# Layer norms of the batch after next taken in the fourth group, the next batch's q and k tiles a step sooner, and the openings' rows moved by ScalarE and SyncE side by side

## The chip, the cores and the metric

One NeuronCore of a Trainium2 chip runs the whole program. The metric is the device time of one execution in microseconds. The engines are TensorE (PE, with its weight loads PEld), VectorE (DVE), ScalarE (ACT), GpSimd (POOL) and SyncE (SP); SP, ACT and POOL also issue DMAs.

## The reference, cut to what matters

Input x is 4 batches of 512 tokens of 288 channels. Three transformer layers run one after the other, with a small rotation of the channels between the second and the third.

```python
mod = silu(c) @ w_adaln + b_adaln           # shift, scale, gate for attention and for the MLP
h   = (1 + sc_msa) * layernorm(x) + sh_msa
q, k, v = split_heads(h @ w_qkv + b_qkv)    # 16 heads of 18
o   = softmax(q @ k.T * 18 ** -0.5) @ v
x   = x + g_msa * (o @ w_proj + b_proj)
h   = (1 + sc_mlp) * layernorm(x) + sh_mlp
x   = x + g_mlp * mlp(h)                    # first layer: 4 experts, top 2; the others dense, 288 -> 1152 -> 288
```

## The kernel before

Everything is float32, with each large product made of high and low float32r parts. Attention is worked per layer, batch (0 to 3) and group of four heads (0 to 3). A group has four steps, one for each 128 keys. In each step `walk` calls on every engine the same sequence: two heads' tiles, place A, the other two heads' tiles, place B, the products of the step before with v, place C. The places hold everything that isn't a score tile, and `other_work` says what stands in which: "T1" turns the layer-normed rows `xn` of the next batch (PE L1065; ACT then makes `hTraw` and `hTh`, DVE `hTl`), "P" makes one of five tiles of the next batch's q and k rows (PE L1025, ACT L1513 the high part, DVE L1952 the low part), "V" makes v, "R" turns the maxima, "ot" turns the attention's output, "pj" is the projection, "LN1" and "LN2" are the layer norms (statistics on DVE, the rest on POOL, which writes the one buffer `xn`), "HH" is one Householder reflection of the rotation, which POOL works on beside the first two layers.

The softmax needs each row's maximum before the scores are exponentiated. So q k^T is made twice: the "max" tiles (PE L1123, reduced by DVE at L1970) run two groups ahead of the score tiles (PE L1136, exponentiated by ACT at L1560). While group 2 of a batch is scored, the maxima of group 0 of the next batch are found. Their q and k come through DRAM: SP stores the high and the low part of a tile in `qk_rows` (L494) and, when two tiles have landed, loads them stacked into `qs` and `ks` (L511, eight DMAs; "stack" g is for group g and needs tiles g and g + 1). SP works in the order of its code, and the negated maxima (`nmT` to `qs`, L518) go through the same queue.

Each layer opens without this overlap: T1, four P tiles, four V tiles, in the first and third layer also the rest of the modulation and its two gate rows (`gate_out`, ACT L1447, one row buffer `tmpx` in the third layer), and then the maxima of groups 0 and 1. In the opening the PSUM banks go round a ring of seven (`AROUND`). Where gate rows are made, the ring gives their two banks to the sixth and the seventh max tile, which therefore wait for ACT's copy of a gate row.

Of the kernel before, what the change touches and what calls it, by code (L numbers as in the profile page):

```python
# [78 lines left out]
def residuals_before(l):  # L79

    return TT * (0, 2, 2 + B)[l]
# [33 lines left out]
def other_work(g, kt, place, l, b):  # L115
    prev, nxt = b > 0, b + 1 < B
    work = {}
    for kt_, p, w in (
# [4 lines left out]
        0: [(0, "B", [("LN1a", 0)]), (0, "C", [("V", 0)]), (1, "A", [("LN1b", 0)]), (1, "B", [("V", 1)]), (1, "C", [("LN1c", 0)]),  # L123
            (2, "A", [("V", 2)]), (2, "C", [("V", 3)])] if b else
# [10 lines left out]
    for kind, arg in work.get((kt, place), []):  # L135
# [6 lines left out]
        if kind[:3] in ("T1", "LN1") and not nxt:  # L142
            continue
        if not b and g == 1 and (kind == "T1" or kind == "P"):
            continue
# [118 lines left out]
def bass_cond_seq_kernel(nc, a, out):  # L264
# [8 lines left out]
    with ExitStack() as ctx:  # L273
# [172 lines left out]

        @block.sync
        def _(sp):
# [19 lines left out]
            for l in range(NL):  # L468
# [17 lines left out]
                def store_tile(i, tile):  # L486
# [5 lines left out]
                    for part, done in enumerate(("hi_done", "lo_done")):  # L492
                        sp.wait_ge(S[done], i * QT + tile + 1)
                        sp.dma_start(qkd[o:o + QR[tile] // HD, part], qk[0:QR[tile], tile % 2, part, :].bitcast(F32)).then_inc(S[f"qk_st{tile % 2}"], 16)  # L494

                def stack(i, g):

                    if g == 0:
                        store_tile(i, 0)
                    store_tile(i, g + 1)  # L500
# [4 lines left out]
                    o = 2 * HG * g  # L505
                    for to, row, src in ((qs, 0, qkd[o:o + HG]), (qs, 2 * HD, qkd[o:o + HG, 0:1]), (ks, 0, qkd[o + HG:o + 2 * HG, 0:1]),
                                         (ks, HD, qkd[o + HG:o + 2 * HG])):
                        for e in range(2):
                            part = src.rearrange("(p e) a d n -> e (a d) p n", e=2)[e]
                            at = HALF * e + row  # L510
                            sp.dma_start(to[at:at + part.shape[0], i % 2, 2 * g:2 * g + 2, :].bitcast(F32), part).then_inc(S[f"stack_ld{g}"], 16)  # L511
# [15 lines left out]
                for b in range(B - 1):  # L527
                    for g in range(NG):
# [16 lines left out]
                        if g == 0 and b == 0:  # L545
                            stack(B * l, NG - 1)
# [1869 lines left out]
```

## Time and profile before

| what | value |
|---|---|
| median of 3 runs | 1769.82 us (1766.54 to 1772.14) |
| the profiled execution | 1758.09 us, of it 1756.3 us between first and last instruction |
| PE busy | 1604.5 us, 91% |
| DVE, ACT, POOL busy | 1100.8, 943.3 and 607.3 us |

The profiled execution is 11.7 us shorter than the median of the runs. A busy PE in such a page is not a PE at its peak, since pipelined matmuls are counted to their modelled ends; its idle time and the rows that say what ended it are read instead.

### The profile page before, as it was taken

What the parts mean: (1) busy time and instruction counts of PE and PEld (TensorE: products, weight loads), DVE (VectorE), ACT (ScalarE), POOL (GpSimd) and SP (SyncE); (2) the same over time, 40 slices, a digit from 0 to 9 for tenths busy, and PEclk for the clock granted to TensorE, in tenths of its full rate; (3) what the DMA queues carried; (4) which work ended last, traced back from release to release, by engine and by line L of the source; (5) the groups of instructions that cost most, each with busy time, mean ns of one, the idle gap of its engine ahead of it and who ended that gap; (6) DMA issues with size and microseconds to landing.
All of it is one profiled execution on the core that took longest, in us unless ns stands there. A gap on an engine that the chain in (4) does not pass through costs nothing.

```text
span 1756.3 us, 27872 instructions
## 1 busy us (share of the span) xinstructions
PE 1604.5 (91%) x9533; PEld 1050.5 (60%) x9533; DVE 1100.8 (63%) x2234; ACT 943.3 (54%) x1698; POOL 607.3 (35%) x1349
## 2 busy tenths in 40 slices
PE   6899989998989998998799899999987999998998
PEld 5334455446778887877335444479854454543897
DVE  4757667746545446473787777554457877784544
ACT  2466535565555455553366657744432766676442
POOL 1255665665255547572374552110001011201100
PEclk9799989999999999998699999999997999999999
DMA  6652423433373454441442212220204323222000
GB/s 196 194 138 89 155 101 123 163 110 120 120 246 130 142 184 144 156 143 41 143 127 81 93 58 90 72 59 1 46 4 131 99 81 93 67 91 72 18 28 28
DMA packets 100976, 183.44 MB, mean 104 GB/s; under 512 B 12078, under 2 KB 54457, under 8 KB 100723
## 3 DMA queue, kind: packets, MB, share of 16 engines
q1 hardware_dynamic: 90094, 145.97, 26.2%
q0 software_dynamic: 8352, 33.20, 6.1%
q10 hardware_dynamic: 2388, 2.48, 0.5%
q8 instruction: 77, 1.26, 0.3%
q14 instruction: 65, 0.52, 0.1%
HBM read 133.18 MB, written 60.05 MB: 110 GB/s over the span
## 4 chain that ended last, share of the span: by engine, by line
PE 63%; DMA 11%; DVE 9%; ACT 6%; issue 5%; SPq 3%; POOL 2%; ACTq 0%; DVEq 0%; POOLq 0%
PE ps L1284 13%; PE ps L1295 13%; PE ps L1147 7%; PE ps L1136 6%; PE ps L1025 5%; DMA qk_rows<-qk 4%; PE ps L1123 3%; DVE mx L1970 3%; PE ps L1076 3%; PE ps L1032 2%; DMA w2raw<-in_w 2%; ACT pT L1560 2%; SPq L511 2%; PE ps L1065 2%; DMA ks<-qk_rows 1%
## 5 line engine op out<-in xcount | busy, mean ns | idle before, releaser
L1970 DVE TENSOR_REDUCE mx<-ps 128x1 f32<-128x512 f32 x768 | 481.5, 681 | 70.9 <-PE ps L1123 68.7
L1560 ACT ACTIVATE pT<-ps 128x512 f32<-128x512 f32 x768 | 410.5, 601 | 190.5 <-PE ps L1136 189.8
L1123 PE MATMUL ps<-ks,qs 54*128 54x512 f32 x768 | 292.2, 489 | 39.4 <-DMA ks<-qk_rows 32.5
L1136 PE MATMUL ps<-qs,ks 56*128 56x512 f32 x768 | 274.4, 462 | 13.3 <-DMA qs<-nmT 4.7
L1904 DVE TENSOR_TENSOR gl<-gf,gh 128x512 fp32r<-128x512 f32 x171 | 118.8, 696 | 192.5 <-ACT gh L1474 191.4
L1136 PEld LDWEIGHTS ps<-qs,ks 56*128 56x128 f32 x768 | 119.0, 192 | 179.3 <-issue 98.4
L1147 PE MATMUL ps<-pT,vaug 128*32 128x512 f32 x1536 | 213.8, 625 | 5.9 <-ACT pT L1560 5.8
L1295 PE MATMUL ps<-w2h,gh 128*128 128x288 f32 x684 | 207.6, 304 | 2.8 <-DVE tmpx L2004 1.9
L1295 PE MATMUL ps<-w2l,gh 128*128 128x288 f32 x684 | 202.9, 297 | 0.0
L1295 PE MATMUL ps<-w2h,gl 128*128 128x288 f32 x684 | 202.2, 296 | 0.0
L753 POOL TENSOR_SCALAR nwp<-mvp 128x4 f32<-128x4 f32 x21 | 4.5, 212 | 543.8 <-DVE mvp L1791 543.6
L1123 PEld LDWEIGHTS ps<-ks,qs 54*128 54x128 f32 x768 | 124.3, 201 | 74.1 <-DMA ks<-qk_rows 37.3
L1295 PEld LDWEIGHTS ps<-w2h,gh 128*128 128x128 f32 x684 | 130.2, 190 | 10.6 <-issue 3.4
L1295 PEld LDWEIGHTS ps<-w2l,gh 128*128 128x128 f32 x684 | 130.5, 191 | 4.9
L1295 PEld LDWEIGHTS ps<-w2h,gl 128*128 128x128 f32 x684 | 130.2, 190 | 0.0
L1473 ACT ACTIVATE gf<-ps,b1t 128x512 f32<-128x512 f32 x99 | 67.7, 684 | 105.9 <-PE ps L1284 105.8
L1473 ACT ACTIVATE gf<-ps,cols 128x512 f32<-128x512 f32 x72 | 49.6, 689 | 126.4 <-PE ps L1284 126.1
L724 POOL TENSOR_TENSOR hs<-hR,hs 96x1 f32<-96x1 f32 x64 | 42.6, 666 | 208.7 <-ACT hR L1479 208.6
L1284 PE MATMUL ps<-hTh,w1h 128*128 128x512 f32 x252 | 105.0, 417 | 1.4 <-DVE hTl L1928 1.4
L1284 PE MATMUL ps<-hTl,w1h 128*128 128x512 f32 x252 | 100.9, 400 | 0.0
L1284 PE MATMUL ps<-hTh,w1l 128*128 128x512 f32 x252 | 100.7, 400 | 0.0
L1952 DVE SCALAR_TENSOR_TENSOR qk<-ps,cols,qk 126x512 fp32r<-126x512 f32 (+1 forms) x60 | 45.0, 750 | 87.8 <-ACT qk L1513 87.1
(292 smaller groups left out, 3076.5 us busy)
## 6 DMA issues: line engine op xcount, KB each, us to landing
qk_rows<-qk SPq DMA_DIRECT2D x96, 252.0 KB
w1raw<-in_w SPq DMA_DIRECT2D x39, 576.0 KB, 4.2
w2raw<-in_w SPq DMA_DIRECT2D x39, 432.0 KB, 4.9
qs<-qk_rows SPq DMA_DIRECT2D x96, 144.0 KB
ks<-qk_rows SPq DMA_DIRECT2D x96, 144.0 KB
expert_out<-expert_out POOLq DMA_DIRECT2D x8, 1152.0 KB, 6.2
htok<-expert_rows SPq DMA_DIRECT2D x11, 768.0 KB, 6.8
qs<-qk_rows SPq DMA_DIRECT2D x96, 72.0 KB
```

Source lines behind the costliest of these rows:

```text
L1025: ins = mm(ps[0:rows, n, :], w[:, c, o:o + rows], h[:, c, :], start=(c == 0 and k == 0), stop=(c == KC - 1))
L1076: ins = mm(ps[:, n, 0:C], oT[0:k, c, t * P:(t + 1) * P], wproj[0:k, c, :], start=(c == 0), stop=(c == KC - 1))
L1123: ins = mm(bank(n), qs[at:at + KMAX, buf, h // 2, qt * P:(qt + 1) * P], ks[at:at + KMAX, buf, h // 2, :], start=True, stop=True, tile_posi ...
L1136: ins = mm(bank(n), ks[at:at + KROW, b % 2, h // 2, kt * P:(kt + 1) * P], qs[at:at + KROW, b % 2, h // 2, :], start=True, stop=True, tile_ ...
L1147: ins = mm(ps[32 * i:32 * i + 32, 4, :], vaug[:, kt, g % NG * HG + i, :], pT[:, kt % 2 * HG + i, :], start=(kt == 0), stop=(kt == TT - 1), ...
L1284: ins = mm(bank(j % 3), w[:, c, o:o + P], h[:, c, :], start=(c == 0 and n == 0), stop=(c == KC - 1))
L1295: ins = mm(ps[:, 4 + t, 0:C], g[:, j % 3, t * P:(t + 1) * P], w[:, j, :], start=(j == 0 and n == 0), stop=(j == NJ - 1 and n == 2))
L1473: A(gf[:, j % 3, :], bank(j % 3), gelu, bias=bias)
L1560: A(pT[:, kt % 2 * HG + i, :], bank(BANK[when[0], "score", (g, kt, i)]), ACT.Exp, scale=SCALE).then_inc(S["exp_done"], 1)
L1904: V.tensor_tensor(gl[:, j % 3, :], gf[:, j % 3, :], gh[:, j % 3, :].bitcast(F32), ALU.subtract).then_inc(S["gl_done"], 1)
L1952: V.scalar_tensor_tensor(out=qk[0:rows, slot, 1, :], in0=ps[0:rows, BANK[when[0], "P", tile], :], scalar=cols[0:rows, l, tile:tile + 1], i ...
L1970: V.tensor_reduce(mx[:, g % NG, qt, column(i):column(i) + 1], bank(BANK[when[0], "max", (g, qt, i)]), AX.X, ALU.max).then_inc(S["mx_done"], 1)
```

## The change

Three things change. First, in batches 1 and 2 the T1 turns for the next batch leave group 1 and stand in group 0 (steps 2 and 3), the V tiles of group 0 move up a little, and P 0 and P 1 stand in step 0 of group 1 instead of step 1. For this the layer norm must be ready earlier: it is taken in group 3 for the batch after next (batches 0 and 1 do it) instead of in group 0 for the next one (batches 1 and 2). Second, SP stores tiles 0 and 1 ahead of the maxima of group 2. Third, in the openings ACT stores the high parts of tiles 0 to 3 and loads the q half of stacks 0 and 1, while SP stores the low parts and loads the k half; the ones rows (`put_ones`) go to the queue later.

```diff
     own = {
-        0: [(0, "B", [("LN1a", 0)]), (0, "C", [("V", 0)]), (1, "A", [("LN1b", 0)]), (1, "B", [("V", 1)]), (1, "C", [("LN1c", 0)]),
-            (2, "A", [("V", 2)]), (2, "C", [("V", 3)])] if b else
+        0: [(0, "C", [("V", 0)]), (1, "A", [("V", 1)]), (1, "C", [("V", 2)]), (2, "A", [("V", 3)]), (2, "B", [("T1", 0)]), (2, "C", [("T1", 1)]),
+            (3, "B", [("T1", 2)])] if b else
            [(0, "B", [("T1", 0)]), (0, "C", [("T1", 1)]), (1, "A", [("T1", 2)]), (1, "C", [("P", 0)]), (2, "C", [("P", 1)])],
-        1: [(0, "A", [("T1", 0)]), (0, "B", [("T1", 1)]), (0, "C", [("T1", 2)]), (1, "A", [("P", 0)]), (1, "B", [("P", 1), ("pj", 0)]),
+        1: [(0, "A", [("P", 0)]), (0, "C", [("P", 1)]), (1, "B", [("pj", 0)]),
...
-            (2, "C", [("T0", 1)]), (3, "A", [("T0", 2)]), (3, "B", [("pos", 0)])],
+            (2, "C", [("T0", 1)]), (3, "A", [("T0", 2)]), (3, "B", [("pos", 0)]), (0, "B", [("LN1a", 0)]), (1, "A", [("LN1b", 0)]), (1, "C", [("LN1c", 0)])],
...
-        if kind[:3] in ("T1", "LN1") and not nxt:
+        if kind == "T1" and not nxt or kind[:3] == "LN1" and b + 2 >= B:
...
                 G0 = NG * B * l
                 sp.wait_ge(S["oT_ones"], l + 1)
+                store_tile(B * l, 0, (1,))
+                store_tile(B * l, 1, (1,))
+                stack(B * l, 0, (1,))
+                store_tile(B * l, 2, (1,))
+                stack(B * l, 1, (1,))
                 put_ones(0)
+                store_tile(B * l, 3, (1,))
+                stack(B * l, 2)
                 put_ones(1)
-                stack(B * l, 0)
-                stack(B * l, 1)
-                stack(B * l, 2)
...
+                        if g == 1 and b:
+                            store_tile(i, 0)
+                            store_tile(i, 1)
...
                     for tile in range(QT - 1):
                         high_part(it, tile)
+                        act.wait_ge(S["hi_done"], it * QT + tile + 1)
+                        act.dma_start(*rows_of(tile, 0)).then_inc(S[f"qk_st{tile % 2}"], 16)
+                        if tile % 2:
+                            g = tile // 2
+                            for n in (g, g + 1):
+                                act.wait_ge(S[f"qk_st{n % 2}"], stored(it, n))
+                            load_rows(act, it, g, 0)
                     if l != 1:
                         for u in range(2):
                             gate_out(l, u, BANK[when[0], "G", (l, u)])
```

The first place is ACT's queue in the opening of the third layer, from the third high part on. Before, these rows stand there:

```order
L1513 ACTIVATE qk<-ps,cols 126x512 [waits qk_st0,qk_mm]
L1513 ACTIVATE qk<-ps,cols 126x512 [waits qk_st1,qk_mm]
L1447 ACTIVATE tmpx<-ps 4x288 [waits mod_stored1,gate_mm]
L1449 DMA mod_rows<-tmpx 4x288 [waits gate_cp]
L1447 ACTIVATE tmpx<-ps 4x288 [waits mod_stored2,gate_mm]
L1449 DMA mod_rows<-tmpx 4x288 [waits gate_cp]
```

After, with the loads of `qs` for stack 0 (second half of them) ahead of the third high part and those for stack 1 ahead of the gate rows:

```order
L459 DMA qs<-qk_rows 36x2x512
L459 DMA qs<-qk_rows 18x2x512 x2
L1534 ACTIVATE qk<-ps,cols 126x512 [waits qk_st0,qk_mm]
L1647 DMA qk_rows<-qk 7x18x512 [waits hi_done]
L1534 ACTIVATE qk<-ps,cols 126x512 [waits qk_st1,qk_mm]
L1647 DMA qk_rows<-qk 7x18x512 [waits hi_done]
L459 DMA qs<-qk_rows 36x2x512 [waits qk_st0,qk_st1]
L459 DMA qs<-qk_rows 36x2x512
L459 DMA qs<-qk_rows 18x2x512 x2
L1468 ACTIVATE tmpx<-ps 4x288 [waits mod_stored1,gate_mm]
L1470 DMA mod_rows<-tmpx 4x288 [waits gate_cp]
L1468 ACTIVATE tmpx<-ps 4x288 [waits mod_stored2,gate_mm]
```

Both gate rows now stand behind a wait for rows stored in DRAM (`qk_st0`, `qk_st1`), and so does the third high part.

The second place is ACT's queue in the third layer, batch 1, where group 0 ends and group 1 begins (`hTraw` and `hTh` are T1's, `oT` is "ot", `oc` closes the group before, `qk` is a P tile). Before:

```order
L1535 ACTIVATE hTraw<-ps,modcol 128x512
L1540 ACTIVATE hTh<-hTraw 128x512
L1552 ACTIVATE oc<-ps 128x512
L1535 ACTIVATE hTraw<-ps,modcol 128x512
L1540 ACTIVATE hTh<-hTraw 128x512
L1560 ACTIVATE pT<-ps 128x512 x2
L1520 ACTIVATE nmT<-ps 8x512
L1513 ACTIVATE qk<-ps,cols 126x512
L1560 ACTIVATE pT<-ps 128x512 x2
L1513 ACTIVATE qk<-ps,cols 126x512
```

After:

```order
L1556 ACTIVATE hTraw<-ps,modcol 128x512
L1561 ACTIVATE hTh<-hTraw 128x512
L1567 ACTIVATE oT<-ps 96x512
L1581 ACTIVATE pT<-ps 128x512 x2
L1534 ACTIVATE qk<-ps,cols 126x512
L1581 ACTIVATE pT<-ps 128x512 x2
L1573 ACTIVATE oc<-ps 128x512
L1534 ACTIVATE qk<-ps,cols 126x512
L1581 ACTIVATE pT<-ps 128x512 x2
L1541 ACTIVATE nmT<-ps 8x512
```

The T1 pairs now stand ahead of `oc`, in group 0 and among its `oT` copies, and the two P rows follow within the first step of group 1.

The third place is SP's queue in group 1 of the third layer, batch 1. Before:

```order
L518 DMA qs<-nmT 2x2x512 [waits nmT_ready]
L518 DMA qs<-nmT 2x2x512
L494 DMA qk_rows<-qk 7x18x512 [waits hi_done,stack_ld0]
L494 DMA qk_rows<-qk 7x18x512 [waits lo_done]
L494 DMA qk_rows<-qk 7x18x512 [waits hi_done,stack_ld1,stack_ld0]
L494 DMA qk_rows<-qk 7x18x512 [waits lo_done]
L511 DMA qs<-qk_rows 36x2x512 [waits st_mm,qk_st1,qk_st0]
L511 DMA qs<-qk_rows 36x2x512
```

After:

```order
L508 DMA qk_rows<-qk 7x18x512 [waits hi_done,stack_ld0]
L508 DMA qk_rows<-qk 7x18x512 [waits lo_done]
L508 DMA qk_rows<-qk 7x18x512 [waits hi_done,stack_ld1,stack_ld0]
L508 DMA qk_rows<-qk 7x18x512 [waits lo_done]
L524 DMA qs<-nmT 2x2x512 [waits nmT_ready]
L524 DMA qs<-nmT 2x2x512
L459 DMA qs<-qk_rows 36x2x512 [waits st_mm,qk_st1,qk_st0]
L459 DMA qs<-qk_rows 36x2x512
```

The four stores moved ahead of the two DMAs of maxima; the loads stayed behind both.

## Rows read from the trace of the kernel before

**Rows 1.** Waits of PE: engine and line, waited for: total us, times, longest us.

```profile
PE ps L1123 <- DMA ks<-qk_rows: 32.5, 12, 9.3
...
PE ps L1025 <- DVE hTl L1961: 4.1, 5, 0.9
```

**Rows 2.** Busy time by stretch: groups 1 and 2 together (four times), group 0, group 3.

```profile
core 0: us, PE busy (x) PEld busy (x) DVE busy (x) ACT busy (x) POOL busy (x), PEclk, DMA share, GB/s
944.10:988.40 44.30, 40.28 (x231) 20.91 (x230) 30.69 (x61) 28.19 (x54) 25.37 (x80) 1.00 0.24 77
1020.10:1067.00 46.90, 44.72 (x231) 22.76 (x230) 31.02 (x61) 28.55 (x54) 24.00 (x77) 0.89 0.23 72
1429.80:1475.10 45.30, 41.10 (x223) 21.25 (x222) 30.85 (x61) 27.56 (x50) 4.40 (x9) 0.92 0.25 75
1505.40:1547.30 41.90, 39.17 (x221) 19.91 (x221) 30.73 (x61) 27.42 (x50) 4.41 (x9) 1.00 0.25 81
1488.30:1505.40 17.10, 17.00 (x118) 9.10 (x114) 15.50 (x36) 10.60 (x21) 4.40 (x9) 1.00 0.24 71
1547.30:1560.60 13.30, 13.16 (x85) 5.30 (x81) 11.50 (x22) 9.88 (x20) 0.00 (x0) 1.00 0.35 108
```

**Rows 3.** Busy time by stretch, ten us around a stack wait in layer 2.

```profile
1044.00:1054.00 10.00, 8.80 (x30) 3.94 (x27) 5.72 (x15) 3.42 (x7) 7.92 (x23) 0.59 0.13 38
```

**Rows 4.** Chain that ended last, third layer, batch 2, groups 1 and 2: start, us.

```profile
1515.20 1.65 PE ps L1025 x7
...
1518.44 6.13 DMA qk_rows<-qk
...
1527.21 3.85 DMA ks<-qk_rows
...
1531.11 0.51 PE ps L1123 x2
...
1539.14 0.59 PE ps L1065 x4
```

**Rows 5.** Timeline of ACT, third layer, batch 2, start of group 1.

```profile
1507.75 0.63 ACT L1540 ACTIVATE hTh<-hTraw 128x512 fp32r<-128x512 f32 x1
1508.29 1.07 ACT L1560 ACTIVATE pT<-ps 128x512 f32<-128x512 f32 x2
1509.24 0.78 ACT L1535 ACTIVATE hTraw<-ps,modcol 128x512 f32<-128x512 f32 x1
```

**Rows 6.** Timeline of SP's queue, opening of the third layer.

```profile
1325.13 1.47 SPq L511 DMA_DIRECT2D qs<-qk_rows  x4
...
1334.83 1.45 SPq L511 DMA_DIRECT2D qs<-qk_rows  x4
```

**Rows 7.** Timeline of ACT, the same opening.

```profile
1325.16 0.69 ACT L1513 ACTIVATE qk<-ps,cols 126x512 fp32r<-126x512 f32 x1 [2.18 <-DMA qk_rows<-qk]
1328.62 0.40 ACT L1447 ACTIVATE tmpx<-ps 4x288 f32<-4x288 f32 x1 [2.78 <-PE ps L939]
...
1333.22 0.40 ACT L1447 ACTIVATE tmpx<-ps 4x288 f32<-4x288 f32 x1 [4.19 <-DMA mod_rows<-tmpx]
```

**Rows 8.** Timeline of DVE, the same opening.

```profile
1325.88 0.75 DVE L1952 SCALAR_TENSOR_TENSOR qk<-ps,cols,qk 126x512 fp32r<-126x512 f32 x1 [2.12 <-ACT qk L1513]
1326.54 1.54 DVE L1983 TENSOR_TENSOR vaug<-ps,vbias 128x288 f32<-128x288 f32 x4
...
1328.36 1.53 DVE L1786 BATCH_NORM_STATS2 stats<-xres 128x6 f32<-128x288 f32 x4
...
1332.09 9.65 DVE L1970 TENSOR_REDUCE mx<-ps 128x1 f32<-128x512 f32 x16 [1.68 <-PE ps L1123]
```

**Rows 9.** Timeline of PE, the same opening.

```profile
1333.67 4.74 PE L1123 MATMUL ps<-ks,qs 54*128 54x512 f32 x10 [1.15 <-ACT tmpx L1447]
```

**Rows 10.** Timeline of DVE, opening of the second layer.

```profile
841.25 9.65 DVE L1970 TENSOR_REDUCE mx<-ps 128x1 f32<-128x512 f32 x16 [2.51 <-PE ps L1123]
...
852.51 0.69 DVE L1970 TENSOR_REDUCE mx<-ps 128x1 f32<-128x512 f32 x1 [1.19 <-PE ps L1123]
```

More of the change, by code:

```diff
@@ L141, in other_work @@
             continue
-        if kind[:3] in ("T1", "LN1") and not nxt:
+        if kind == "T1" and not nxt or kind[:3] == "LN1" and b + 2 >= B:
             continue
-        if not b and g == 1 and (kind == "T1" or kind == "P"):
+        if not b and g == 1 and kind == "P":
             continue
@@ L445, in load_ada, with rows_of, load_rows @@
             eng.dma_start(to[CW:CW + 1, KC - 1, at:at + n * C], a["w_ada"][l][C:C + 1, src]).then_inc(S[sem], 16)
+        def rows_of(tile, part):
+            return qkd[HT * tile:HT * tile + QR[tile] // HD, part], qk[0:QR[tile], tile % 2, part, :].bitcast(F32)
+        def load_rows(eng, i, g, which):
+            o = 2 * HG * g
+            for to, row, src in (((qs, 0, qkd[o:o + HG]), (qs, 2 * HD, qkd[o:o + HG, 0:1])),
+                                 ((ks, 0, qkd[o + HG:o + 2 * HG, 0:1]), (ks, HD, qkd[o + HG:o + 2 * HG])))[which]:
+                for e in range(2):
+                    part = src.rearrange("(p e) a d n -> e (a d) p n", e=2)[e]
+                    at = HALF * e + row
+                    eng.dma_start(to[at:at + part.shape[0], i % 2, 2 * g:2 * g + 2, :].bitcast(F32), part).then_inc(S[f"stack_ld{g}"], 16)
         @block.sync
@@ L484, in _, with store_tile @@
                     sp.wait_ge(S["ys_done"], 16 * TILES)
-                def store_tile(i, tile):
+                def store_tile(i, tile, parts=(0, 1)):
                     o = HT * tile
@@ L491, in store_tile, with stack @@
                             sp.wait_ge(S[f"stack_ld{g}"], i * 128)
[L492 to L500, printed above, removed]
+                    for part in parts:
+                        sp.wait_ge(S[("hi_done", "lo_done")[part]], i * QT + tile + 1)
+                        sp.dma_start(*rows_of(tile, part)).then_inc(S[f"qk_st{tile % 2}"], 16)
+                def stack(i, g, which=(0, 1)):
                     for tile in (g, g + 1):
@@ L504, in stack @@
                         sp.wait_ge(S["st_mm"], NU * (NG * (i - 2) + g + 1))
[L505 to L511, printed above, removed]
+                    for part in which:
+                        load_rows(sp, i, g, part)
                 def maxima(G, g):
@@ L521, in _ @@
                 sp.wait_ge(S["oT_ones"], l + 1)
+                store_tile(B * l, 0, (1,))
[3 more added lines that the diff above has]
+                stack(B * l, 1, (1,))
                 put_ones(0)
+                store_tile(B * l, 3, (1,))
+                stack(B * l, 2)
                 put_ones(1)
[L524 to L526 removed]
                 for b in range(B - 1):
+                    i = b + (B * l + 1)
                     for g in range(NG):
@@ L774, in others @@
                         if kind == "LN1c":
-                            normalise(1, it + 1, b + 1, EPS[l], (("tr1_done", it * KC + KC), ("tr2_done", it * KC + KC)))
+                            normalise(1, it + 2, b + 2, EPS[l], (("tr1_done", it * KC + 2 * KC), ("tr2_done", it * KC + 2 * KC)) + ((("lg_tr", it),) if l == 0 and b else ()))
                         elif kind == "LN2c":
@@ L1615, in start @@
                         split_high(c, it)
+                    if l:
+                        act.wait_ge(S["fc2_mm"], NJ * units_before(l) + 3)
+                        act.wait_ge(S["xm_done"], residuals_before(l))
+                        for g in range(NG):
+                            act.wait_ge(S[f"stack_ld{g}"], it * 128)
+                    if l == 2:
+                        act.wait_ge(S["xr_done"], TT * B)
                     for tile in range(QT - 1):
                         high_part(it, tile)
+                        act.wait_ge(S["hi_done"], it * QT + tile + 1)
[5 more added lines that the diff above has]
+                            load_rows(act, it, g, 0)
                     if l != 1:
@@ L2030, in others @@
                         elif kind[:3] == "LN1":
-                            statistics(1, it + 1, b + 1, kind[3])
+                            statistics(1, it + 2, b + 2, kind[3])
                         elif kind == "pj":
```

15 lines of the change are left out of this document (11 added, 4 removed).

## The prediction

> **What bounds the kernel now.** I read the waits of TensorE first, then the busy time by stretch, then the chain that ended last, then the timelines of the openings. Among the waits one is far ahead: TensorE's max tiles wait 32.5 us in 12 places for rows of q and k that come back from DRAM [rows 1]. They fall in two kinds of places. In the three openings nothing hides the way through DRAM, and in batches 1 and 2 of the second and third layer the maxima of the next batch's group 0 start group 2, and its rows have just been asked for. The chain shows why: P 1 ends 1.65 us after 1515.20, then come high part, low part and SP's store, 6.13 us until the store has landed, eight loads, 3.85 us until the last one has landed, and the max tile at 1531.11 [rows 4]. From P 1's end to that tile are 14.3 us, whatever TensorE does meanwhile. Groups 1 and 2 together take 44.3, 46.9, 45.3 and 41.9 us in these four batches, with the same instructions on TensorE but for the reflections of the second layer [rows 2]. Part of the spread is the clock: around one of the waits the granted clock was 0.59, so for much of these ten us TensorE stood at 1.2 GHz, after it had idled [rows 3].
>
> **The change part by part, groups 1 and 2.** P 1 moves from the second step of group 1 to its first. Before it stand now two pairs of tiles, P 0, v's products and P 1 itself, an estimated 6.2 us from the group's start; with the 14.3 us of the chain the stack is there at 20.5 us. Without T1 the group's own work is about 20.7 us, so at most some tenths of a wait remain. To price it I start at the calmest batch, 41.9 us at full clock [rows 2]. The gap between the last load's issue, its 3.85 us, and the tile [rows 4] left TensorE idle for 1.7 us; that goes. T1 is three turns of 0.59 us, read at a turn of the same shape [rows 4], 1.8 us. P 0 no longer waits for `hTl`, five such waits of 0.8 us on the average, and its surroundings [rows 1], 1.0 us. So 41.9 - 1.7 - 1.8 - 1.0 = 37.4 us, and the same for the third layer's batch 1, since it has the same work. In the second layer I add 1.5 us, as POOL's reflections there hold TensorE in group 2 whatever the rows do: 38.9 us. Gains: 44.3 - 38.9, 46.9 - 38.9, 45.3 - 37.4, 41.9 - 37.4, together 25.8 us. The first layer had no such wait, and I set its groups 1 against its groups 0 and 3 at nothing (bounds -4 and +4): its batches are slowed by other work.
>
> **Group 0.** It gets T1: 1.8 us on TensorE, which was already busy for 17.00 of 17.10 us [rows 2]. On ScalarE each turn costs 0.78 + 0.63 us [rows 5], three of them 4.2 us, and all three stand in the second half of the group beside eight exponentials of 0.54 us (4.3 us) and the `oT` copies. That is more than the 8.5 us of half a group, so exponentials and with them v's products come late. I take 2.4 us for each of four batches, 9.6 us. Lower bound 1.0 (TensorE's gap at the start of the group swallows part), upper bound 4.2 (ScalarE's work in full).
>
> **Group 3.** The statistics, 1.53 us for four [rows 8] and 0.4 us for their aggregation, move to group 3 in batches 0 and 1. DVE was busy for 11.50 of 13.30 us there [rows 2] and each max tile needs it; it was busy for 15.50 of 17.10 us in group 0 too, but there `hTl` takes the place of the statistics. I take 1.0 us for each of four groups, 4.0 us, between 0 and 2. POOL's part is hidden by two or three steps in which nobody asks for `xn`.
>
> **The openings.** The low part of tile 1 sets the landing, and it is made no sooner, so the stores gain nothing (in the second layer the four DMAs of ones no longer stand ahead of them, about 1 us). The loads do: q's four cost 1.47 us of issuing ahead of k's four [rows 6], and now both go side by side. But ScalarE now stands in this queue. From the landing, 1325.13 in the third layer, it issues loads for 1.5 us, then makes the third high part, stores it, makes the fourth, 3.8 us in all. DVE follows with the low part (0.75), v (1.54), the modulation (0.5) and the statistics (1.9) [rows 8] and reaches the first maximum 8.6 us after the landing, at 1333.7 instead of 1332.09. These 1.6 us I take for the first layer too.
>
> The third layer loses more. The sixth and seventh max tile need the banks of the gate rows. The seventh already waited 1.15 us for the second copy [rows 9], because both copies share one row buffer and 4.19 us pass until the first has landed [rows 7]. Now both stand behind the second wait for stored rows. Low part 2 is made at 1328.1, the store lands some 6.4 us later, 1334.5; loads to 1336.0, first gate 1336.4, its row landed 1340.7, second gate 1341.1, seventh max tile and DVE from 1341.5. Ten more reductions of 0.6 us end at 1347.6 instead of 1341.75: 5.9 us later, and DVE is what the steps behind wait for. In the second layer there are no gates: DVE starts about 0.9 us sooner, and the 1.19 us for stack 1 [rows 10] vanish, 2.0 us gained. Openings: 1.6 - 2.0 + 5.9 = +5.5 us, between 0 (if the second landing is quick) and +9.
>
> The Trainium skill (Trainium Kernel Development and Optimization, Key Constraints) says that DMAs of all issuing engines run on the same 16 DMA engines and that several issuers only save "the sequencer's issue time". By that rule the gain of an opening is one times 1.47 us as above, and the sum stays; were the landings halved as well, each opening would be some 3 us better. No row here shows two queues at once on these rows.
>
> **Sum.** -25.8 + 9.6 + 4.0 + 5.5 = -6.7 us. On the profiled execution that is 1758.1 - 6.7 = 1751.4 us. The median of the runs shown lies 11.7 us above that execution; with the same difference taken off, 1769.8 - 6.7 = 1763.1 us.
>
> **The rivals.**
> *The openings don't lose.* If the second landing takes 4 us instead of 6.4 and the gate row's 2 instead of 4.2, the third opening costs 1.3 us and the first nothing: 5 to 6 us less, 1757 us. For it: those landings were timed with other rows in flight. Against: they still are. Chance 0.17.
> *Nothing is left.* Work moves between groups, and where DVE and TensorE were both nearly full it comes back in full: groups 0 at 4 us, groups 3 at 1.2 make +20.8 instead of +13.6, sum 0, 1770 us. For it: TensorE busy for 17.00 of 17.10 us. Against: groups 1 were full as well and lose the same work. Chance 0.16.
> *Slower, by ScalarE in group 0.* T1's copies stand among exponentials that feed v's products, DVE waits for `hTh` ahead of the maxima, and the ring of banks fills. It happens in batches 1 and 2 of all three layers, so six times. Beyond my 2.4 us each further us costs 6 us; from 4.4 us a group on the whole is slower by over 0.3%, at 5 us it gives 1769.8 - 6.7 + 6 x 2.6 = 1779 us. For it: 8.5 us of ScalarE and more in 8.5 us. Against: the same copies stood in one step and a half of group 1 before. Chance 0.17.
> *The forecast*, between -13 and -1 us: 0.50.
>
> **How the numbers follow.** A measurement of this kernel tells about 0.3%, 5.3 us, from no change. The forecast lies just beyond it: of its 0.50 some 0.32 is faster and 0.17 within. The first rival is faster. "Nothing is left" gives 0.03 faster, 0.10 within, 0.03 slower; the slower rival 0.13 slower, 0.04 within. Together faster 0.53, within 0.30, slower 0.17. The range takes the first rival's end and half of the slower one: 1751 to 1776 us.
>
> **What would show it.** Right: the stack waits at the start of group 2 gone and the granted clock there near 1.00; groups 1 and 2 at 37 to 39 us; groups 0 at 19 to 20 us; in the third opening DVE idle for about 3.5 us after its sixth reduction, with the second `tmpx` copy near 16 us after the first landing. Wrong: a wait for `ks` still standing in group 2 (P 1 came not soon enough, or the store took longer), idle time of TensorE at v's products in group 0, or waits for `nmT` at the start of group 3, since group 2 is now short and SP brings the maxima behind stack 1's loads.

## The result, and the profile after

The changed kernel takes 1786.56 us (median of 4 runs, 1784.34 to 1789.86) where the kernel before took 1770.43 us beside it: ratio 1.0096, 95% interval 1.0073 to 1.0119. That is 17 us slower, outside the range on record (1751 to 1776 us), and the other way than forecast. A second set of runs, on another chip, gave 1.0097 (1.0056 to 1.0138).

The two profiled executions lie 31.8 us apart (spans 1756.3 and 1788.1 us), because the one of before was the fastest seen by then and the one of the change the slowest of its four. So the rows say where time is spent, the ratios how much counts. A second profile of before, below, helps to tell a draw from an effect.

Engine totals on the page after the change: TensorE is busy for 25 us more with the same 9533 matmuls, the first sign of a lower clock.

```profile
PE 1629.5 (91%) x9533; PEld 1057.9 (59%) x9533; DVE 1103.6 (62%) x2234; ACT 945.0 (53%) x1698; POOL 610.0 (34%) x1349
```

The waits of TensorE, changed kernel (engine and line, waited for: total us, times, longest us):

```profile
PE ps L1144 <- DMA qs<-qk_rows: 12.4, 3, 8.6
PE ps L999 <- POOL hr L731: 9.9, 3, 3.9
...
PE ps L1144 <- ACT tmpx L1468: 9.1, 2, 6.1
```

The max tiles' 32.5 us in 12 places [rows 1] have become 12.4 us in 3, all in openings: the stack waits at the start of group 2 are gone, as forecast. But these four waits were only 6.9 of the 32.5 us; the rest belonged to the openings. Here they are on TensorE's timeline of the kernel before, the second layer's two and the third layer's two:

```profile
969.61 0.50 PE L1123 MATMUL ps<-ks,qs 54*128 54x512 f32 x2 [0.94 <-DMA ks<-qk_rows]
1045.88 0.80 PE L1123 MATMUL ps<-ks,qs 54*128 54x512 f32 x2 [1.20 <-DMA ks<-qk_rows]
1456.96 0.80 PE L1123 MATMUL ps<-ks,qs 54*128 54x512 f32 x2 [3.13 <-DMA ks<-qk_rows]
1531.11 0.51 PE L1123 MATMUL ps<-ks,qs 54*128 54x512 f32 x2 [1.67 <-DMA ks<-qk_rows]
```

Two other waits stand out in the changed kernel: 9.9 us for `hr`, which is POOL's part of a reflection, and 9.1 us for `tmpx`, the gate rows. In the kernel before they were:

```profile
PE ps L978 <- POOL hr L710: 2.1, 1, 2.1
...
PE ps L1123 <- ACT tmpx L1447: 1.1, 1, 1.1
```

Busy time by stretch, changed kernel: groups 1 and 2 together of the same four batches as [rows 2], then group 0 and group 3 of the third layer, and group 0 of the first layer's batch 1.

```profile
core 0: us, PE busy (x) PEld busy (x) DVE busy (x) ACT busy (x) POOL busy (x), PEclk, DMA share, GB/s
965.70:1012.00 46.30, 42.81 (x219) 21.55 (x218) 29.50 (x58) 24.59 (x49) 24.20 (x77) 0.89 0.24 73
1048.30:1091.90 43.60, 40.43 (x217) 20.64 (x216) 28.49 (x57) 24.32 (x48) 22.24 (x73) 0.96 0.24 78
1467.90:1506.70 38.80, 37.67 (x209) 18.76 (x208) 29.62 (x59) 23.66 (x44) 4.41 (x9) 1.00 0.28 87
1540.10:1578.40 38.30, 37.58 (x209) 18.73 (x208) 29.15 (x58) 23.54 (x44) 4.41 (x9) 1.00 0.28 88
1520.20:1540.10 19.90, 19.07 (x130) 10.38 (x126) 15.58 (x30) 14.60 (x27) 0.00 (x0) 1.00 0.20 61
142.30:170.80 28.50, 23.75 (x132) 12.33 (x128) 17.24 (x40) 15.12 (x29) 17.27 (x43) 0.82 0.34 106
1506.70:1520.20 13.50, 13.02 (x79) 5.42 (x79) 12.51 (x30) 9.69 (x19) 4.42 (x9) 1.00 0.36 106
```

The third layer came to 38.8 and 38.3 us at a full clock (forecast 37.4). The second layer came to 46.3 and 43.6 us, at a clock of 0.89 and 0.96 (forecast 38.9). POOL is busy for over 22 us there (24 and 25 us before [rows 2]), for 4.4 us in the third layer: what it does more in the second layer are the reflections.

**Where POOL holds TensorE.** POOL's timeline of the changed kernel, at the turn from batch 0 to batch 1 in the first layer: the end of one reflection, the layer norm "LN1c", the next reflection's first and last step.

```profile
133.62 0.31 POOL L731 TENSOR_TENSOR hr<-hp 96x59 f32<-96x59 f32 x1
135.81 0.20 POOL L774 TENSOR_SCALAR nwp<-mvp 128x4 f32<-128x4 f32 x1 [1.88 <-DVE mvp L1826]
...
137.81 2.28 POOL L781 TENSOR_SCALAR xn<-xres,nwp 128x288 f32<-128x288 f32 x4
140.16 0.51 POOL L784 COPY xn<-xn 128x384 f32<-128x384 f32 x1
140.64 0.56 POOL L745 TENSOR_TENSOR hs<-hR,hs 96x1 f32<-96x1 f32 x1
...
147.47 0.30 POOL L731 TENSOR_TENSOR hr<-hp 96x58 f32<-96x58 f32 x1
```

The product that hands this reflection over on TensorE, ScalarE's copy of it for POOL, and TensorE's next product of a reflection:

```profile
136.78 0.46 PE L999 MATMUL ps<-hr,ones 96*96 96x128 f32 x2
...
137.63 0.29 ACT L1500 ACTIVATE hR<-ps 96x128 f32<-96x128 f32 x1
...
147.88 0.71 PE L999 MATMUL ps<-hr,ones 96*96 96x128 f32 x2 [3.92 <-POOL hr L731]
```

The copy was there at 137.92. POOL was free at 133.93, waited 1.88 us for the statistics of the layer norm, which stands ahead of the reflection in its code, and took up the reflection at 140.64, 2.7 us late. The layer norm takes 4.8 us, a reflection 7.1 us, and two steps of group 3 about 7 us: TensorE stands still for 3.92 us, and the stretch behind runs at a mean clock of 0.82. In the kernel before the same product waited 1.5 us, for DVE.

In group 2 of the second layer's batch 1 the pattern is the same, but the layer norm in it is LN2c, which the change did not move. POOL's row 991.14 is its start, 995.99 and 1001.74 are the next reflection's first and last step:

```profile
991.14 0.20 POOL L774 TENSOR_SCALAR nwp<-mvp 128x4 f32<-128x4 f32 x1
...
995.99 0.56 POOL L745 TENSOR_TENSOR hs<-hR,hs 96x1 f32<-96x1 f32 x1
...
1001.74 0.20 POOL L731 TENSOR_TENSOR hr<-hp 96x9 f32<-96x9 f32 x1
```

```profile
1002.04 0.71 PE L999 MATMUL ps<-hr,ones 96*96 96x128 f32 x2 [3.15 <-POOL hr L731]
```

This product is the one that waited 2.1 us before (at 982.3 us in that trace). The third wait for `hr`, 2.8 us, is its counterpart in batch 2.

**Where the gate rows hold DVE.** The third opening on ScalarE, to set beside [rows 7]:

```profile
1350.30 1.57 ACTq L459 DMA_DIRECT2D qs<-qk_rows  x4
1351.97 0.69 ACT L1534 ACTIVATE qk<-ps,cols 126x512 fp32r<-126x512 f32 x1 [8.72 <-issue]
...
1361.01 1.54 ACTq L459 DMA_DIRECT2D qs<-qk_rows  x4
1362.65 0.40 ACT L1468 ACTIVATE tmpx<-ps 4x288 f32<-4x288 f32 x1 [8.43 <-issue]
...
1369.53 0.40 ACT L1468 ACTIVATE tmpx<-ps 4x288 f32<-4x288 f32 x1 [6.48 <-DMA mod_rows<-tmpx]
```

The same stretch on DVE, to set beside [rows 8]:

```profile
1359.65 3.08 DVE L2005 TENSOR_REDUCE mx<-ps 128x1 f32<-128x512 f32 x5 [0.86 <-PE ps L1144]
1363.93 0.69 DVE L2005 TENSOR_REDUCE mx<-ps 128x1 f32<-128x512 f32 x1 [1.19 <-PE ps L1144]
1370.81 4.28 DVE L2005 TENSOR_REDUCE mx<-ps 128x1 f32<-128x512 f32 x7 [6.18 <-PE ps L1144]
```

DVE idles where it was forecast to, after its sixth maximum, but for 6.18 us instead of 3.5. The second copy stands 19.2 us behind the first loads (1369.53 against 1350.30); 16 us was forecast. A second profile of the changed kernel (after_2 below) has 18.2 us there, with 5.72 us in place of the 6.48.

### The profile page after: what moved, and what is told of

It reads as the page before. It is cut to its first block, busy times and chain, and to the rows that moved or that the text cites. A ratio compares the mean times of both kernels' runs of the same rounds, so it can differ in the third digit from the quotient of the medians.

```text
span 1788.1 us, 27886 instructions
## 1 busy us (share of the span) xinstructions
PE 1629.5 (91%) x9533; PEld 1057.9 (59%) x9533; DVE 1103.6 (62%) x2234; ACT 945.0 (53%) x1698; POOL 610.0 (34%) x1349
## 4 chain that ended last, share of the span: by engine, by line
PE 63%; DVE 11%; DMA 9%; ACT 6%; issue 4%; POOL 4%; SPq 2%; ACTq 1%; another core or an unknown queue 0%; DVEq 0%; POOLq 0%
PE ps L1305 12%; PE ps L1316 12%; PE ps L1168 7%; PE ps L1157 6%; PE ps L1046 5%; DVE mx L2005 5%; PE ps L1097 4%; DMA qk_rows<-qk 4%; PE ps L1144 3%; DMA w2raw<-in_w 2%; PE ps L1053 2%; PE ps L1086 2%; ACT qk L1534 1%; PE ps L1067 1%; PE ps L1060 1%
## 5 line engine op out<-in xcount | busy, mean ns | idle before, releaser
L1144 PE MATMUL ps<-ks,qs 54*128 54x512 f32 x768 | 300.6, 492 | 33.2 <-DMA qs<-qk_rows 12.4
L1157 PE MATMUL ps<-qs,ks 56*128 56x512 f32 x768 | 278.3, 463 | 16.0 <-DMA qs<-nmT 4.4
L1168 PE MATMUL ps<-pT,vaug 128*32 128x512 f32 x1536 | 218.1, 633 | 6.6 <-ACT pT L1581 6.6
L1144 PEld LDWEIGHTS ps<-ks,qs 54*128 54x128 f32 x768 | 126.1, 202 | 73.5 <-DVE mx L2005 23.5
```

What stands on the lines that cost most here:

```text
L1144: ins = mm(bank(n), qs[at:at + KMAX, buf, h // 2, qt * P:(qt + 1) * P], ks[at:at + KMAX, buf, h // 2, :], start=True, stop=True, tile_posi ...
L1157: ins = mm(bank(n), ks[at:at + KROW, b % 2, h // 2, kt * P:(kt + 1) * P], qs[at:at + KROW, b % 2, h // 2, :], start=True, stop=True, tile_ ...
L1168: ins = mm(ps[32 * i:32 * i + 32, 4, :], vaug[:, kt, g % NG * HG + i, :], pT[:, kt % 2 * HG + i, :], start=(kt == 0), stop=(kt == TT - 1), ...
```

## The experiments

The tables below give the time from the first score tile of a group to that of the next, read in each kernel's timeline. Ratios are to the kernel before on the same chip. The median of the kernel before moved between 1762 and 1774 us from chip to chip, so only ratios are compared. Each interval reaches 0.2 to 0.4% to either side, and a difference of two ratios is uncertain by an estimated 0.3 to 0.5%: many of the conclusions rest on the traces, and the ratios say whether they add up.

**The kernel before again.**

> The kernel before, unchanged, for a second profile of it and for the spread: ratio 1.000 within 0.003. If the profiled execution shown in front (11.7 us below the median of the runs) was a lucky one, this profile has its stack waits in the same 12 places but a span near 1768 us.

Ratio 0.9990 (0.9958 to 1.0022), the profiled span 1760.9 us, again at the low end of its runs: the page's execution was no great exception. It waits 23.6 us in 10 places for stacks, where the same 12 places had been expected. The group times of the two profiles show what is fixed and what is a draw. In the second layer group 1 of batch 2 took 24.1 us in both; group 2 took 20.2 and 23.2 us in batch 1, 22.8 and 19.9 us in batch 2; group 0 of the first layer's batch 3 took 17.6 and 21.1 us. So [rows 2] had bad draws, and the first layer's 17.6 us was a good one.

**The openings alone.** The order of work of before, with the third part of the diff only:

```diff
+                store_tile(B * l, 0, (1,))
+                store_tile(B * l, 1, (1,))
+                stack(B * l, 0, (1,))
...
-                put_ones(1)
-                stack(B * l, 0)
-                stack(B * l, 1)
...
```

> The kernel before with only the third change: in the openings ScalarE stores the high parts and loads the q half of stacks 0 and 1, SyncE the rest, ones rows later. Order of work in the groups and of stores there as before. Theory one (the openings cost what the two traces show between T1 and the first score tile: +2.9, -1.3 and +10.6 us): about 12 us slower than before, 9 to 15; in the third layer the second gate row is copied some 19 us after the first loads are issued, and DVE is idle for over 5 us among the maxima of group 0. Rival (most of the loss comes from the moved work, and what an opening loses comes back behind it): at most 5 us slower.

Ratio 1.0042 (1.0019 to 1.0065), 7.5 us, which lies between both theories, and 1.0063 (1.0027 to 1.0098), 11 us, on another chip, which lies within the first. From the first maximum to the first score tile the third opening took 25.4 and 26.1 us, against 17.9 and 18.4 in the two profiles of before. The second opening got no slower.

**The moved work alone.** The table of places and the order of stores as in the change, the opening as before:

```diff
-                        act.dma_start(*rows_of(tile, 0)).then_inc(S[f"qk_st{tile % 2}"], 16)
-                        if tile % 2:
...
-                            load_rows(act, it, g, 0)
```

> The changed kernel with the opening of the kernel before: SyncE alone stores and loads, ones rows first. Theory one (openings cost 12 of the 16 us): 2 to 6 us slower than before, since what groups 1 and 2 gain (11 us by the traces) is lost again in groups 0 and 3 and by reflections that wait for GpSimd. Rival one (the forecast's own terms without the openings): 12 us faster. Rival two (the moved work is the cause): over 9 us slower.

Ratio 1.0048 (1.0029 to 1.0067), 8.5 us, more than theory one's 2 to 6 us and just under rival two. 0.42% and 0.48% add up to nearly all of the 0.96%: two faults, about equal as far as the intervals tell, that hardly meet. Here the waits for `hr` are 9.9 us, as in the changed kernel.

**Gate rows freed.** ScalarE no longer waits for stack 1's rows:

```diff
-                stack(B * l, 1, (1,))
+                stack(B * l, 1)
...
-                        if tile % 2:
-                            g = tile // 2
+                        if tile == 1:
+                            g = 0
```

> The changed kernel, but ScalarE loads only the q half of stack 0; SyncE loads stack 1 in full, so that in the first and third layer the gate rows no longer stand behind a wait for stack 1's stored rows. Theory one (that wait holds the gate rows, and these the sixth and seventh max tile): the first gate row is copied as soon as TensorE has made it, the third opening is 5 to 9 us shorter, and the kernel 5 to 9 us faster than the changed one, 7 to 11 us slower than before. Rival (the landing of the first gate row, 6.5 us, is what counts, wherever it starts): 0 to 3 us faster than the changed one.

Ratio 1.0053 (1.0027 to 1.0080), 0.43% or 7.6 us under the changed kernel, as theory one has it. ScalarE and DVE in the third opening:

```profile
1345.08 1.57 ACTq L459 DMA_DIRECT2D qs<-qk_rows  x4
...
1351.36 0.40 ACT L1468 ACTIVATE tmpx<-ps 4x288 f32<-4x288 f32 x1 [2.35 <-PE ps L960]
...
1356.31 0.40 ACT L1468 ACTIVATE tmpx<-ps 4x288 f32<-4x288 f32 x1 [4.54 <-DMA mod_rows<-tmpx]
```

```profile
1354.49 9.65 DVE L2005 TENSOR_REDUCE mx<-ps 128x1 f32<-128x512 f32 x16 [0.92 <-PE ps L1144]
```

The second copy is made 11.2 us behind the first loads instead of 19.2, and DVE reduces all sixteen tiles in one go. First maximum to first score tile: 18.4 us, as before, against 26.0 us in the changed kernel.

**Do the 7 us count?** The same cure on the openings alone:

> The kernel before with the new openings, but ScalarE loads only the q half of stack 0. Order of work and reflections as before. Theory (two queues at once save an opening nothing that counts; the gate rows were all of the openings' loss in the third layer): maximum to first score tile in the third opening 18.4 us again (25.4 with the fault), time within 4 us of before. Rival (sharing the queues gains 1.5 us an opening once the gate rows are free): 3 to 5 us faster than before.

Ratio 1.0037 (1.0012 to 1.0062), only 0.05% under the openings alone on the other chip, though its third opening took 18.4 us. At 6.5 us over before it was a miss, so four kernels were run side by side on one chip.

> The changed kernel again, on one chip with the next three, to settle what the openings cost. Ratio to before 1.008 to 1.011 in either theory; its maximum to first score tile in the third opening takes 25 to 26 us.

> The changed kernel with the gate rows free of the wait for stack 1, again. Theory (the 7 us which the trace shows in the third opening are in the time in full): 0.3 to 0.5% under the changed kernel of the same call. Rival (part of them is given back by shorter groups behind the opening): under 0.2%.

> Only the new openings, again. Theory (openings cost the gate rows' 7 us and a little): 0.4 to 0.6% over before. Its partner is the next kernel, which had 1.0037 on another chip where this one had 1.0042; if the 7 us count in full they must lie 0.3 to 0.5% apart here.

> Only the new openings, with the gate rows free, again. Theory (the 1.0037 was a draw at the edge of its interval): 1.000 to 1.002. Rival (beside the gate rows the new openings cost something else, some 5 us, that no row has shown yet): 1.003 or more again.

Measured: 1.0097, 1.0044 (1.0013 to 1.0075), 1.0063, 1.0027 (0.9996 to 1.0057). The two differences are 0.53% and 0.36%, 9 and 6 us. With the 0.43% and the 0.05% of the earlier pairs the mean is 0.34%, 6 us: the gate rows' 7 us of the trace count, most of them at least; whether in full the intervals don't tell. Open_free's second ratio lies between its theory (up to 1.002) and its rival (1.003). Whether the new openings cost a little beside the gate rows (0.27% and 0.37% in these two, 0.05% where the moved work stands beside them) stays open; no gain of theirs shows in any ratio.

**Reflections made cheap.** In both kernels eight steps of POOL's reflection are left out or replaced, so that the rotation becomes the identity and the kernels compute without it:

```diff
-                step(g.tensor_tensor(nrm, sig, half, ALU.pow))
-                step(g.tensor_scalar(sg, al, 0.0, 2.0, ALU.is_ge, ALU.mult))
-                step(g.tensor_scalar(sn, sg, nrm, nrm, ALU.mult, ALU.subtract))
+                step(g.tensor_scalar(sn, al, 0.0, 1.0, ALU.mult, ALU.mult))
...
-                    step(g.tensor_tensor(rest, rest, outer(row, RD - 1 - j), ALU.subtract))
```

> The kernel before with a shorter reflection on GpSimd: eight of its steps are left out or replaced by a multiplication by zero, so the rotation becomes the identity; everything else stands. A control for the next kernel. GpSimd's part of a reflection falls from about 6.5 to 4 us. Theory (reflections bind a few places before too, such as the 2.1 us at 982.3): 3 to 10 us faster than before. Rival: nothing waits for them: within 3 us.

> The changed order of work with the opening of before and the same shorter reflection. Theory one (the layer norm moved into group 3 stands on GpSimd between two reflections, and group 2, now free of its wait for the stack, waits for GpSimd instead): against the kernel before with the same shorter reflection it is no slower, -4 to +2 us, where with full reflections it was 8.5 us slower; TensorE's waits for GpSimd (3 to 4 us each) are gone. Rival (the loss is ScalarE's and TensorE's, by the layer-norm turns in group 0): still 6 to 10 us slower than that control.

Ratios 0.9907 (0.9873 to 0.9941) and 0.9899 (0.9865 to 0.9933). The control's 16 us were far more than the 3 to 10 expected: reflections cost the kernel before more than its one wait of 2.1 us for `hr` shows. With full reflections the moved work was 0.48% slower than its control, with short ones it is 0.08% faster. Its waits for `hr` are gone. The second layer, groups 1 and 2 of batch 1 and group 2 of batch 2, first of the control and then with the moved work:

```profile
943.20:967.30 24.10, 23.33 (x128) 12.88 (x126) 17.63 (x33) 15.20 (x29) 4.91 (x18) 1.00 0.24 76
967.30:985.50 18.20, 17.20 (x106) 8.28 (x102) 13.12 (x29) 12.85 (x26) 8.39 (x27) 1.00 0.28 85
...
1041.30:1059.60 18.30, 17.25 (x108) 8.32 (x104) 13.14 (x29) 12.88 (x26) 8.25 (x27) 1.00 0.28 88
```

```profile
948.50:970.70 22.20, 22.20 (x118) 11.61 (x116) 16.10 (x31) 11.48 (x24) 4.12 (x18) 1.00 0.28 88
970.70:987.80 17.10, 16.75 (x108) 8.09 (x104) 13.07 (x29) 12.73 (x25) 8.39 (x27) 1.00 0.29 84
...
1045.10:1062.20 17.10, 16.74 (x108) 8.07 (x104) 13.07 (x29) 12.72 (x25) 8.25 (x27) 1.00 0.29 85
```

Group 2 falls to the 17.1 us of the third layer, and groups 1 and 2 to 39.3 us, the forecast's 38.9 almost. But the control, with its stack wait in place, needs only 42.3 us. Its group 2 takes 18.2 us against 17.1, both at a clock of 1.00: there the wait was worth 1.1 us, not 5 to 8. In the third layer, without any reflection, group 2 took 17.8 to 21.8 us in 14 instances of the old order and 16.9 to 17.7 us in 22 with the early P tiles: there it was worth 3 us on the mean, the fall of the clock included (0.84 in the 21.7 us of the kernel before).

**Reflections moved.** The moved work with full reflections at other steps:

```diff
-FWD_STEP = {(0, 0): (2, 5, 7, 9, 11, 14), (0, 1): (0, 2, 5, 7, 10, 12, 14), (0, 2): (0, 2, 5, 7, 10, 12, 14), ...
-            (1, 1): (0, 2, 4, 6, 8, 10, 12), (1, 2): (0, 2, 4, 6, 8, 10, 12)}
+FWD_STEP = {(0, 0): (2, 5, 7, 9, 11, 14), (0, 1): (1, 3, 5, 7, 10, 12, 14), (0, 2): (1, 3, 5, 7, 10, 12, 14), ...
+            (1, 1): (0, 2, 4, 7, 10, 12, 14), (1, 2): (1, 3, 5, 7, 10, 12, 14)}
```

> The changed order with the opening of before and full reflections, but where batches take a layer norm in group 3 the reflections stand at other steps (in the first layer's batches 1 and 2 and the second layer's batch 2 at 1, 3, 5, 7, 10, 12, 14, in its batch 1 at 0, 2, 4, 7, 10, 12, 14). Theory one (GpSimd's chain of reflection, layer norm, reflection is what group 2 and the start of the next batch wait for): 5 to 9 us faster than with the old steps, so 0 to 4 us slower than before. Rival (GpSimd only shares the blame with the turns in group 0): 0 to 3 us faster than with the old steps.

Ratio 0.9993 (0.9963 to 1.0023), 0.55% or 9.7 us under the same kernel with the old steps, which ran on another chip; theory one had 5 to 9 us. The wait that is left, in the list of waits:

```profile
PE ps L999 <- POOL hr L731: 3.7, 2, 2.0
```

The kept traces say the same of the second layer without any ratio. From the first score tile of batch 1 to that of batch 3 it takes 151.6 to 154.7 us in the eight profiles with the old order and full reflections at the old steps, 157.3 to 161.3 us in the five with the moved order, 154.9 and 155.1 us where the reflections are shifted too (moves_shift and repaired), and 148.1 and 148.6 us in the two short kernels. Shifted steps with the old order were run for the second layer alone (third_shift below, 151.8 and 151.6 us); what they would give the old order in the first layer was not run.

**Both repairs.** Gate rows freed and reflections moved, the rest as in the change.

> The whole change with both repairs: ScalarE loads only the q half of stack 0 (so that the gate rows are free), and the reflections stand at the shifted steps. Theory (the two faults add up, 0.43% for the gate rows and 0.55% for the reflections, and are all of the change's 0.96%): 1.000 of before, 0.996 to 1.003. Rival (they overlap, since each also lowers the granted clock where the other waits): 1.004 or more.

Ratio 0.9998 (0.9974 to 1.0022): within 0.24% the two faults are the whole of the 0.96%, and what is left of the change neither gains nor loses.

**The third layer alone.** The order of work chosen per layer:

```diff
+    early = l == 2
...
-        1: [(0, "A", [("P", 0)]), (0, "C", [("P", 1)]), (1, "B", [("pj", 0)]),
+        1: ([(0, "A", [("P", 0)]), (0, "C", [("P", 1)]), (1, "B", [("pj", 0)])] if early else
+            [(0, "A", [("T1", 0)]), (0, "B", [("T1", 1)]), (0, "C", [("T1", 2)]), (1, "A", [("P", 0)]), (1, "B", [("P", 1), ("pj", 0)])]) + [
```

> The changed order of work in the third layer alone; first and second layer and all openings as before. No reflections run in the third layer. Theory one (the moved work gains where no reflection stands beside it: layer 3 took 266.8 us before and 262.5 us with the moves): 3 to 6 us faster than before. Rival (group 0's loss cancels the gain there too): within 2 us of before.

Ratio 0.9997 (0.9968 to 1.0026), so not told from no change, nor from the low end of the 3 to 6 us expected. Its third layer took 262.3 us, against 266.9 and 266.6 in the profiles of before. The same without the earlier P tiles:

```diff
-        1: ([(0, "A", [("P", 0)]), (0, "C", [("P", 1)]), (1, "B", [("pj", 0)])] if early else
+        1: ([(1, "A", [("P", 0)]), (1, "B", [("P", 1), ("pj", 0)])] if early else
```

> In the third layer alone the layer norms and the T1 turns are moved as in the change, but P 0 and P 1 stay in the second step of group 1. Theory (only the earlier P tiles shorten group 2; the turns cost group 0 a little more than they give back in group 1): batches 1 and 2 of the third layer have groups 0 of 19.8 us, groups 1 of 21 to 22, and groups 2 still wait for the stack and take 18 to 21 us, so the layer takes 267 to 270 us. Rival (a shorter group 1 without T1 is what counts): groups 2 at 17 us without any earlier P.

Ratio 0.9997 (0.9970 to 1.0024), third layer 262.8 us. The layer's expected 267 to 270 us was a miss. Batch 1, groups 0, 1 and 2:

```profile
1418.60:1438.40 19.80, 18.97 (x128) 10.36 (x124) 15.53 (x30) 14.53 (x27) 0.00 (x0) 1.00 0.30 91
1438.40:1459.00 20.60, 20.60 (x113) 11.06 (x111) 15.82 (x30) 11.17 (x22) 0.00 (x0) 1.00 0.28 88
1459.00:1478.20 19.20, 17.80 (x104) 8.19 (x100) 13.57 (x30) 12.68 (x23) 4.41 (x9) 0.91 0.27 82
```

Group 2 still idles for 1.4 us and its clock falls to 0.91, yet the three groups take 59.6 us, against 60.0 us with the early P tiles, whose group 0 was one at a clock of 0.94. Groups 1 and 2 alone take 39.7 us against 39.0 in batch 1 and 38.3 us in either kernel in batch 2. With the turns gone from group 1, P comes early enough by itself for most of the effect; putting it a step sooner is worth under 1 us a batch here.

**A better version?** The third layer's moved work, and the second layer as before but with its reflections at 0, 2, 4, 7, 10, 12, 14.

> The candidate for a better version: the moved work in the third layer alone, and in the second layer, whose work stands as before, the reflections of batches 1 and 2 at steps 0, 2, 4, 7, 10, 12, 14 in place of 0, 2, 4, 6, 8, 10, 12. Theory (third layer 4 us shorter, groups 2 of the second layer 1 to 3 us shorter since TensorE waited for GpSimd there): 5 to 9 us faster than before. Rival (what a group saves there is within the spread of the second layer's batches): 0 to 4 us faster.

> The candidate (moved work in the third layer alone, shifted reflections in the second) once more, since its first interval, 0.9961 to 1.0014, holds both no change and the 5 us expected. Theory: 0.996 to 0.999. Rival: 0.999 or more, and no better version is shown.

Ratios 0.9987 (0.9961 to 1.0014) and 0.9980 (0.9954 to 1.0005), medians of 1757.54 and 1758.18 us beside 1763.25 and 1762.09 us for before. The mean is 0.9983, about 3 us; each interval holds 1, so it is the best candidate and not shown to be faster; the 5 to 9 us expected of it are missed. Its second layer's groups 2 took 18.9 and 18.6 us (before: 20.2 and 23.2, 22.8 and 19.9), but its groups 1 rose from 24.1 to 24.7 us and its groups 3 from 13.8 to 14.6 and 14.4.

| us, group 0 / 1 / 2 | before | before again | changed | moves, short | moves, shifted | third alone |
|---|---|---|---|---|---|---|
| 2nd layer, batch 1 | 17.9 / 24.1 / 20.2 | 18.0 / 24.1 / 23.2 | 21.1 / 22.1 / 24.1 | 21.1 / 22.1 / 17.1 | 21.1 / 22.8 / 20.3 | 18.0 / 24.1 / 20.2 |
| 2nd layer, batch 2 | 17.9 / 24.1 / 22.8 | 17.9 / 24.1 / 19.9 | 22.7 / 22.2 / 21.4 | 21.1 / 22.1 / 17.1 | 20.3 / 22.6 / 18.6 | 18.0 / 24.1 / 19.9 |
| 3rd layer, batch 1 | 17.0 / 23.5 / 21.7 | 17.0 / 23.5 / 21.5 | 19.8 / 21.4 / 17.4 | 19.9 / 21.4 / 17.0 | 21.4 / 21.4 / 17.0 | 21.1 / 21.6 / 17.3 |
| 3rd layer, batch 2 | 17.0 / 23.6 / 18.4 | 17.0 / 23.5 / 20.7 | 19.8 / 21.4 / 17.0 | 19.8 / 21.4 / 17.1 | 19.9 / 21.4 / 17.0 | 19.8 / 21.4 / 17.0 |

## Why the prediction was wrong, step by step

**The steps that failed.** Two steps left out what is queued on POOL. One is the sentence "POOL's part is hidden by two or three steps in which nobody asks for `xn`". It asked who reads what POOL writes, and not what is queued behind it on POOL. Behind LN1c stands a reflection, whose result TensorE asks for in the next batch. In the first layer the layer norm was at a place with room before (three steps between reflections) and now stands between two that are two short steps apart: 3.92 us of waiting where 1.5 us had stood.

The other is the term of 1.5 us a batch for the reflections in group 2 of the second layer. I had seen that these hold TensorE and sized it too small. There the reflection at step 6, LN2c (which was not moved), and the reflection at step 8 follow each other on POOL, and step 10's product waits 3.15 us; the changed kernel lies 7.0 and 4.3 us over the short one there (46.3 and 43.6 against 39.3 twice), where the kernel before lies 2.0 and 4.5 us over its own short control.

Together the reflections' places cost 0.55%, 9.7 us (moves_shift against moves_only, on two chips); cutting POOL's work instead removes 0.56% (the two short kernels against 0.48%). Both figures are uncertain by 0.3 to 0.5%, and the second layer's traces above bear them out. The first layer's share isn't settled: its batch 1 has group 0 at 28.5 us in the changed kernel, 20.6 with the reflections moved, but 26.1 with short ones, where TensorE waits 1.4 us for DVE at the same product and the clock is low as well. So there POOL's length alone is not the cause.

**Groups 1 and 2, -25.8 us.** Measured in the profiled pair -11.4 (178.4 to 167.0). I had read the 32.5 us of [rows 1] as one fault; of them the four waits that the moved work could remove were 0.9, 1.2, 3.1 and 1.7 us. The third layer was right within 1.4 us. In the second the size was wrong at both ends: the 38.9 us were missed by POOL, and the 44.3 and 46.9 us that they were taken from were not the stack wait's doing. The control with short reflections takes 42.3 us with its wait. Over all profiles with full reflections at the old steps, groups 1 and 2 of the second layer take 45.1 us on the mean in the old order and 44.4 in the moved one: 0.7 us gained where 5.4 and 8.0 were forecast. I read 46.9 us beside a clock of 0.59 [rows 3] and gave the whole distance to the wait; the second profile shows that batch at 44.0 us, and the other at 47.3.

**Group 0, +9.6 us.** Right in kind, 13.5 us in the profiled pair (3.2, 4.7, 2.8, 2.8). A group 0 with the turns costs 2.8 to 3.1 us more at full clock, where 2.4 had been taken, and group 1 gives back 2.0 us: moving the turns loses about 1 us a batch by itself. In 9 of 24 such groups of the third layer the clock was 0.92 to 0.94, and they cost 4.1 to 4.4 us (the last section has a row). In the second layer the stack wait, worth 1.1 us, about pays for that; in the third it pays more, and the layer takes about 4 us less on the mean of its profiles. That fits the repaired kernel's 0.9998, which can't tell 4 us from nothing.

**Group 3, +4.0 us.** 0.7 us in the pair (batches 0 and 1 of the second and third layer), within the spread of these groups. DVE had room; the layer norm's price was on POOL.

**The openings, +5.5 us.** The mechanism was right in each part. First maximum to first score tile in the third opening: 26.0 against 17.9 us, where 5.9 had been added for both stretches; by the four pairs of runs the gate rows cost 1 to 9 us, 6 on the mean. The gate row's landing was mis-sized, 6.48 us measured against the 4.19 of [rows 7]. The 1.6 us for the start of the maxima can't be told from the spread (ScalarE's copy of the first turn to the first maximum took 22.8 and 25.0 us in the two profiles of before, 25.3 us after). The second opening took 44.3 us from that copy to its first score tile against 45.5 and 43.3: none of the 2.0 us gained for certain. The rule of the Trainium skill (Trainium Kernel Development and Optimization, Key Constraints) that several issuers only save issuing time is not contradicted: in the new openings the queues issue side by side (1350.30 on ScalarE in the rows above, and this row on SyncE), and the openings with free gate rows are not faster, 1.0037 and 1.0027.

```profile
1350.29 1.44 SPq L459 DMA_DIRECT2D ks<-qk_rows  x4
```

**The slower rival** was given 0.17, by ScalarE in group 0. Slower came true by another mechanism, which no case named: ScalarE's rival needed 4.4 us a group, and the turns cost 2.8 to 3.1 us at full clock. The groups that did cost 4.1 to 4.4 us had TensorE waiting for ScalarE for no more than the others, 0.4 us. What the repaired kernel shows is the other rival, "Nothing is left" (0.16), though not term by term. The chances as written add up to 0.52 faster, 0.31 within and 0.16 slower, not 0.53, 0.30 and 0.17; nothing rests on it.

## What to carry to other kernels

When a piece of work is moved on an in-order engine, ask first what stands behind it in that engine's queue and who waits for that, and only then who reads its own result; look for the gap between its new neighbours in the steps' own lengths. Never price a wait by the distance between two instances of a stretch that also differ in clock: a second profile costs little and shows which times are fixed (24.1 us in both) and which are draws (19.9 to 23.2 us). And an engine that is given transfers to issue carries every wait of those transfers into its compute, here two copies of 0.40 us, for which two banks of the ring had to wait.

## What the runs showed of the hardware

Some groups' times are reproduced to 0.1 us, others differ from one execution to the next with the same instructions. Group 0 of the third layer in the moved order was measured 24 times: 15 took 19.8 or 19.9 us at a granted clock of 1.00, as the row 1520.20 above, and 9 took 21.1 to 21.4 us at 0.92 to 0.94, as this one of moves_only, with the same waits on TensorE (0.4 us for ScalarE, 0.3 us for DVE):

```profile
1426.90:1448.40 21.50, 20.67 (x130) 10.86 (x126) 16.27 (x31) 14.57 (x27) 0.00 (x0) 0.92 0.31 84
```

Single gaps of 2.5 to 4.4 us appear on TensorE in the second layer's batch 0, most often in the last step of group 1 but not in every execution; the records name no releaser, ScalarE or DVE, and the gaps were not explained. From one copy of a gate row (4x288 elements) to the next, ScalarE waited 4.19, 4.54, 5.72 or 6.48 us for the row to land, the two longest in the changed kernel, where two queues had just been issuing a stack's loads; that this is the cause wasn't tested.
